# Audio tower on one core: the matrix work of a group laid out over its half units, the router in single steps

## The reference, cut to what matters

```python
h = tok(x, ...)                       # conv 2 -> 32 channels, width 7; 16 samples folded; 64 x 128 x 256
h = h + mamba(layernorm(h), ...)      # x_inner, z = x @ W_in; conv over 4 steps; silu
                                      # delta = softplus(...); h_t = exp(delta*A) * h_t-1 + delta*B*x
                                      # y = sum_n h*C + D*x; y * silu(z); @ W_out
h = h + moe(layernorm(h), ...)        # 8 experts, the two with the largest softmax gates
                                      # out = sum over the two: gate * (silu(x @ wg) * (x @ wi)) @ wo
```

## Time and profile before

| | us |
|---|---|
| median of 3 runs | 3025.95 (3023.35 to 3029.46) |
| the profiled execution | 3023.12 |
| its span in the profile | 3021.4 |
| busy: TensorE, VectorE, GpSimd, ScalarE | 2618.3, 2159.1, 1727.5, 1470.0 |
| matmuls of the state sums (L1215) | 1053.1 |
| scans (L899), idle just before them | 1172.5, 114.3 |
| products with C (L907) | 625.9 |
| delta*x*B on GpSimd (L514) | 1157.4 |

### The profile page before, as it was taken

One profiled execution on the slowest core, in us unless ns is written; L12 is line 12 of the kernel. 1 busy time (PEld: TensorE's weight loads), 2 busy tenths in 40 slices (PEclk: granted clock), 3 DMA queues, 4 the chain that ended last, 5 costly groups with the idle time before them and its releaser, 6 DMA issues. The chain is left out here.

```text
span 3021.4 us, 29407 instructions
## 1 busy us (share of the span) xinstructions
PE 2618.3 (87%) x7774; PEld 1298.5 (43%) x7775; DVE 2159.1 (71%) x2367; ACT 1470.0 (49%) x2717; POOL 1727.5 (57%) x864
## 2 busy tenths in 40 slices
PE   4689798887979889898888989877569999999999
PEld 2234343343434334343343434333246666666665
DVE  0599998999999999999999999999632222222222
ACT  1665656656566665656666566665212222222222
POOL 1567768677786867768677776877322222222222
PEclk9899998999999999899999989999889999999999
DMA  1321403223040321404123040321522222222222
GB/s 38 127 97 42 145 26 129 75 86 131 23 146 29 132 99 55 143 15 142 60 100 130 24 146 29 129 109 42 188 61 44 44 45 44 44 45 43 44 44 31
DMA packets 125603, 236.12 MB, mean 78 GB/s; under 512 B 46450, under 2 KB 93715, under 8 KB 109123
## 3 DMA queue, kind: packets, MB, share of 16 engines
q1 hardware_dynamic: 98342, 200.56, 19.5%
q0 software_dynamic: 26128, 34.36, 6.6%
q10 hardware_dynamic: 1036, 0.09, 0.0%
HBM read 182.22 MB, written 53.78 MB: 78 GB/s over the span
## 5 line engine op out<-in xcount | busy, mean ns | idle before, releaser
L514 POOL TENSOR_TENSOR arena<-u,arena 128x2048 f32<-128x2048 f32 x256 | 1157.4, 4527 | 368.4 <-DVE psum L899 366.9
L1215 PE MATMUL psum<-hc,ident 128*128 128x512 f32 x2048 | 1053.1, 641 | 263.2 <-DVE hc L907 262.5
L899 DVE TENSOR_TENSOR_SCAN psum<-psum,arena 128x1024 f32<-128x1024 f32 x512 | 1172.5, 2290 | 114.3 <-ACT psum L705 79.4
L1215 PEld LDWEIGHTS psum<-hc,ident 128*128 128x128 f32 x2048 | 382.3, 200 | 817.3 <-DVE hc L907 450.2
L705 ACT ACTIVATE psum<-delta,a_neg 128x508 f32<-128x508 f32 x1024 | 656.5, 674 | 0.6
L907 DVE TENSOR_TENSOR hc<-psum,arena 128x1024 f32<-128x1024 f32 x512 | 625.9, 1222 | 15.4
L588 POOL DMA_INDIRECT out_dram<-hres,tok_id x136 | 211.1, 1552 | 599.2 <-ACT hres L837 549.3
L1346 PE MATMUL psum<-arena,xnt 128*128 x1088 | 514.2, 595 | 0.0
L1101 DVE COPY z<-psum 128x512 f32<-128x512 f32 x136 | 94.0, 691 | 457.5 <-PE psum L1355 457.5
L837 ACT ACTIVATE hres<-psum,tok_w 128x256 f32<-128x256 f32 x136 | 64.4, 473 | 454.4 <-PE psum L1365 447.7
L1365 PE MATMUL psum<-arena,z 128*128 x1088 | 257.1, 379 | 0.9 <-DVE z L1101 0.9
(11 more groups left out here) (145 smaller groups left out, 1923.4 us busy)
## 6 DMA issues: line engine op xcount, KB each, us to landing
arena<-ssm_rows SPq DMA_DIRECT2D x128, 1024.0 KB, 5.8
delta<-expert_rows SPq DMA_DIRECT2D x136, 129.0 KB, 2.1
h_saved_rows<-hnew SPq DMA_DIRECT2D x16, 512.0 KB, 6.7
hres<-h_saved_rows SPq DMA_DIRECT2D x16, 512.0 KB
out_dram<-h SPq DMA_DIRECT2D x16, 512.0 KB, 2.9
draw<-ssm_rows SPq DMA_DIRECT2D x16, 256.0 KB, 3.1
arena<-in_L_ffn_wg_dram SPq DMA_DIRECT2D x8, 512.0 KB
arena<-in_L_ffn_wi_dram SPq DMA_DIRECT2D x8, 512.0 KB
```

Of the source, the lines that this page charges most:

```text
L514: pool.tensor_tensor(dBx[k % 2], rep, b_rep[:, q * QN:(q + 1) * QN, :], ALU.mult).then_inc(dbx_ready, 1)
L899: nc.vector.tensor_tensor_scan(h, h, src, 0.0, ALU.mult, ALU.add).then_inc(scan_done, 1)
L1215: last = nc.tensor.matmul(yacc[(k // HC) % 2], ident[:, :], hc[k % 2][:, i, :], start=False, stop=(k % HC == HC - 1 and i == 1))
```

## The change

TensorE: the first three projections of z of a group move from `k` = 0 to 2 of its own step to `k` = 29 to 31 of the step before (group 0: into the front, ahead of softplus on ScalarE), the fourth from 3 to 1; the output projection moves from 4, 5, 6, 7 to 2, 3, 6, 9; turning of the normed rows from 5, 6 to 3, 4; the first projection of x from 7 to 5 with its convolution at 7 and 8; the turned rows of the second norm from 14, 15 to 17, 18, the logits from 16 to 19, the counts from 21 to 27. ScalarE's evacuations follow; its first norm is cut in two (k = 1 and 2), Silu of z goes from 8 to 9, the four Abs are one per half unit (23 to 26), Exp and Ln go from 26 and 27 to 27 and 28, Relu to 26, 29, 30, 31.

VectorE: the router becomes 19 operations, one or two per half unit from 20 to 29, on both sides of `times_c`; it works on logits less their maximum, the first gate is the reciprocal of the sum of exponentials, the second that times `esecond`, an exponential of the second largest that ScalarE makes (`second_gate`). Its scratch is all in PSUM, over ten slices of `bank_b`. The mask is gone: `count` adds both one-hots (28 matmuls of 8 columns rather than 14). The residual additions stand at 4 and 10 ahead of `times_c`, statistics and their aggregation in different half units.

GpSimd: additions, products and `rsqrt` one per unit, and both scatters of a group are two groups behind (units 2, 3 and 5, 6), so that all scatters of the last group but one move to the tail.

The core of the diff:

```diff
+                pool.wait_ge(second_exp, g + 1)
+                pool.tensor_tensor(row[:, :, C + 1:C + 2], einv[:, :].rearrange("p (b a) -> p b a", a=1),
+                                   esecond[:, :].rearrange("p (b a) -> p b a", a=1), ALU.mult).then_inc(second_set, 1)
...
-                    if k in (0, 1, 4):
-                        c = {0: 1, 1: 2, 4: 3}[k]
+                    if k == 0 and not last:
+                        rsqrt(g + 1, 0, stat1, pow1)
+                    if k in (1, 4, 8):
+                        c = {1: 1, 4: 2, 8: 3}[k]
                         add_delta(g, c)
                         make_u(g, par, c)
                     if not second:
-                        if k == 0:
+                        if k == 2:
+                            first_row(g - 2)
+                        if k in (2, 3):
+                            scatter(g - 2, 0, 2 * (k - 2))
+                        if k == 5:
                             second_row(g - 2)
-                        if k in (1, 2):
-                            scatter(g - 2, 1, 2 * (k - 1))
-                    if k == 0 and not last:
-                        rsqrt(g + 1, 0, stat1, pow1)
-                    if not first:
-                        if k == 5:
-                            rsqrt(g - 1, 1, stat2, pow2)
-                        if k == 12:
-                            first_row(g - 1)
-                        if k in (13, 14):
-                            scatter(g - 1, 0, 2 * (k - 13))
-
-            def tail(g):
-                second_row(g - 1)
-                scatter(g - 1, 1, 0)
-                scatter(g - 1, 1, 2)
-                rsqrt(g, 1, stat2, pow2)
+                        if k in (5, 6):
+                            scatter(g - 2, 1, 2 * (k - 5))
+                    if k == 7 and not first:
+                        rsqrt(g - 1, 1, stat2, pow2)
...
+                nc.scalar.activation(r_ex, r_sub, ACT.Exp).then_inc(lexp_ready, 1)
+
+            def second_gate(g):
+                actq.wait_ge(dv, ROUTER * g + 7)
+                ahead(actq, second_set, g)
+                nc.scalar.activation(esecond[:, :], second[:, :], ACT.Exp).then_inc(second_exp, 1)
...
+                for c in range(NCH - 1):
+                    evac_z(0, c)
+                for c in range(NCH):
+                    softplus_abs(0, c)
...
-                    if k == 31 and not last:
-                        softplus_relu(g + 1, 3)
                     if k + 1 < HU:
                         exps(g, k + 1)
                     elif not last:
+                        softplus_relu(g + 1, 3)
                         exps(g + 1, 0)
-                    if k < NCH:
-                        evac_z(g, k)
+                    if not last and k in (1, 2):
+                        norm1(g + 1, k - 1)
+                    if k == 2:
+                        evac_z(g, 3)
+                    if k == 9:
+                        silu_z(g)
                     if not last:
-                        if k == 3:
-                            norm1(g + 1)
-                        if k in (5, 6):
-                            evac_xnt(g + 1, k - 5)
-                        if k in (7, 10, 13, 16):
-                            evac_xi(g + 1, (k - 7) // 3)
-                        if k in (9, 12, 15, 18):
...
-                    if k == 8:
-                        silu_z(g)
+                        if k in (3, 4):
+                            evac_xnt(g + 1, k - 3)
+                        if k in (5, 10, 13, 16):
+                            evac_xi(g + 1, (5, 10, 13, 16).index(k))
+                        if k in (8, 12, 15, 18):
+                            evac_conv(g + 1, 1 - par, (8, 12, 15, 18).index(k))
                     if not first:
-                        if k in (12, 13):
-                            norm2(g - 1, k - 12)
                         if k in (14, 15):
-                            evac_xn2t(g - 1, k - 14)
-                        if k == 17:
+                            norm2(g - 1, k - 14)
+                        if k in (17, 18):
+                            evac_xn2t(g - 1, k - 17)
+                        if k == 21:
                             router_exp(g - 1)
+                        if k == 26:
+                            second_gate(g - 1)
...
-                        if k in (24, 25):
-                            softplus_abs(g + 1, k - 24)
-                        if k == 26:
+                        if k in (23, 24, 25, 26):
+                            softplus_abs(g + 1, k - 23)
+                        if k == 27:
                             softplus_exp(g + 1)
-                        if k == 27:
+                        if k == 28:
                             softplus_ln(g + 1)
-                            softplus_relu(g + 1, 0)
-                        if k == 28:
-                            softplus_relu(g + 1, 1)
-                            softplus_relu(g + 1, 2)
+                        if k in (26, 29, 30):
+                            softplus_relu(g + 1, (26, 29, 30).index(k))
+                        if k in (29, 30, 31):
+                            evac_z(g + 1, k - 29)
...
+            def first_keys(g):
+                dve.wait_ge(lexp_ready, g + 1)
+                nc.vector.scalar_tensor_tensor(out=r_key, in0=r_sub, scalar=0.0, in1=key_w[:, :, :],
+                                               op0=ALU.is_ge, op1=ALU.mult).then_inc(dv, 1)
+
+            def largest_key(g, n):
+                after(g, n)
+                nc.vector.tensor_reduce(kmax[:, :], r_key, AX_X, ALU.max).then_inc(dv, 1)
+
+            def one_hot(g, n, k, done):
+                after(g, n)
+                nc.vector.tensor_tensor(oh[:, k, :, :], r_key, bc(kmax[:, :]), ALU.is_equal).then_inc(done, 1)
+
+            def without_first(g):
+                after(g, 4)
+                nc.vector.scalar_tensor_tensor(out=r_rest, in0=oh[:, 0, :, :], scalar=-1.0e30, in1=r_sub,
+                                               op0=ALU.mult, op1=ALU.add).then_inc(dv, 1)
+
+            def exp_sum(g):
+                nc.vector.tensor_reduce(esum[:, :], r_ex, AX_X, ALU.add).then_inc(dv, 1)
+
+            def second_max(g):
+                after(g, 5)
+                ahead(dve, second_exp, g)
+                nc.vector.tensor_reduce(second[:, :], r_rest, AX_X, ALU.max).then_inc(dv, 1)
...
+            def exp_inverse(g):
+                after(g, 6)
+                ahead(dve, second_set, g)
+                nc.vector.reciprocal(einv[:, :], esum[:, :]).then_inc(dv, 1)
...
+            def second_equal(g):
+                after(g, 7)
+                nc.vector.tensor_tensor(r_eq, r_rest, bc(second[:, :]), ALU.is_equal).then_inc(dv, 1)
+
+            def second_keys(g):
+                after(g, 9)
+                nc.vector.tensor_tensor(r_key, r_eq, key_w[:, :, :], ALU.mult).then_inc(dv, 1)
...
+                    if not first:
+                        if k == 4:
+                            residual(g - 1, 0)
+                        if k == 10:
+                            residual(g - 1, 1)
+                        if k == 20:
+                            router_max(g - 1)
+                        if k == 22:
+                            first_keys(g - 1)
+                        if k == 23:
+                            one_hot(g - 1, 3, 0, dv)
+                        if k == 24:
+                            second_max(g - 1)
+                            exp_inverse(g - 1)
+                        if k == 25:
+                            second_keys(g - 1)
+                        if k == 26:
+                            one_hot(g - 1, 11, 1, mask_ready)
+                        if k == 28:
+                            positions(g - 1)
+                        if k == 29:
+                            slots(g - 1)
+                    if k == 30 and more:
+                        aggregate(g + 2, 0, stat1)
                     times_c(g, k)
                     if not first:
-                        if k == 6:
-                            residual(g - 1, 0)
-                        if k == 9:
-                            residual(g - 1, 1)
+                        if k == 10:
                             stats2(g - 1)
-                        if k == 17:
-                            router_a(g - 1)
-                        if k in (19, 20):
-                            for part in ((0, 1), (2,))[k - 19]:
-                                router_b(g - 1, part)
+                        if k == 11:
+                            aggregate(g - 1, 1, stat2)
+                        if k == 20:
+                            router_sub(g - 1)
                         if k == 22:
-                            router_c(g - 1)
-                    if k == 28 and more:
+                            largest_key(g - 1, 2)
+                        if k == 23:
+                            without_first(g - 1)
+                            exp_sum(g - 1)
```

(50 more changed lines are left out.)

152 lines of the change are left out of this document (71 added, 81 removed).

## The result

The changed kernel takes **2897.26 us** (median of 4, 2895.21 to 2898.09), the kernel before beside it 3024.65: ratio 0.9578, 95% interval 0.9565 to 0.9591. That is 127 us less; 104 were forecast. 2897 lies in the stated range (2892 to 2974), near its lower end, but outside the 2900 to 2950 that the forecast gave its own sum, and nearer to rival 2 (2894) than to the forecast (2922). The profiled execution took 2897.52 us, its span is 2895.8 (before 3021.4).

A forecast was written before the change was run, and what follows sets the result against it. VectorE was taken to set the scan phase's pace. Front +11, group 0 -3, fourteen middle groups -105 (-7.5 each), last group -7, tail -1.4 and +1.5: -104 from 3025.95, 2922 us; own range 2900 to 2950, with rivals 2892 to 2974.

The forecast's parts named there:

- rival 2: Middle groups: nearly all stalls go, -9.5 us a group, 2894 us in all; chance 0.09.
- the slots' prices: VectorE small operations: 0.23 us when chained, 0.10 apart behind times_c, free between scan and times_c; -4.4 us a group together.
- The stalls at k=4, 8 and 9: Middle groups: k=4 (GpSimd) goes, -1.1 us; k=8 and 9 (TensorE's lag) go, -2.8 us.
- The stall at k=21: Middle groups: the chain around Silu of x stays, uncovered by router work; stall 2.3 us instead of 0.6.
- The front: Before the first scan: three z evacuations ahead of ScalarE's Abs, each behind its matmuls, +11 us.
- Rival 1: Stalls come to as much as before at other places; only VectorE's 4.4 us a group count, 2971 us; chance 0.20.
- rival 3: A small VectorE operation costs 0.23 us wherever it stands; only the six removed count, 2960 us; chance 0.04.
- rival 4: Half clock under z's matmuls from k=29: no change (3025) or slower (+51 us); chance 0.03 same, 0.05 slower.
- The 0.45 at k=26: Middle groups: one Abs instead of two ahead of the exponentials cuts the stall from 1.17 to about 0.45 us.
- The 0.5 for half clock under z: z's matmuls at k=29 to 31 meet half clock at times: 0.5 us a group, bounds 0 and 7.
- the 0.4 of small gaps: Middle groups: small stalls on VectorE left as before, 0.4 us a group.
- the bound of +12: Tail: GpSimd must send eight scatters before rsqrt while weights load; taken as +1.5 us, bounds 0 and +12.

The follow-up runs named there:

- experiment 2: Kernel before with the new router in single steps, nearly all other work in the old order: 2987.93 us, ratio 0.9883.
- experiment 3: Changed kernel with GpSimd's additions and products back at units 0, 1, 4 and first scatters at k=1, 2: 2923.54 us, ratio 0.9670.
- experiment 1: Changed kernel with the same 19 router operations gathered in four blocks behind times_c: 2933.79 us, ratio 0.9703.
- experiment 5: Kernel before with one filler matmul behind the turning of x at k=22 and 23: 3015.81 us, ratio 0.9959, executions in two clusters.
- experiment 8: Changed kernel with SyncE waiting for the earlier groups' scatters before asking for the weights of experts 2 to 8: 2897.8 us, ratio 0.9587.

## Why the prediction came out as it did

**Right.** VectorE sets the pace, and its work went by the slots' prices: the router's share fell from 5.1 to 1.07 us (forecast 1.1). The stalls at k=4, 8 and 9 went with the order that made them (experiment 2; the one at k=4 with GpSimd's part of it, experiment 3). The stall at k=21 came, and with its size: 2.22 for 2.3. The front gave +11.9 for +11, in the way described: two projections of 3.75 and 3.78 us, one of 1.99. Group 0, the last group, the router's chain in the tail (15.70 to 14.32) and the experts came out within half a microsecond each. Rival 1 fails on the stalls (2.45 left of 6.7), rival 3 on experiment 1, rival 4 on the clock, 1.00 from 229 to 1935 us. Rival 2, that nearly all stalls go, has the nearest number (2894, -9.5 us a group for the -9.36 measured) but not the mechanism: the stall at k=21 stayed with 2.2 us, and VectorE's work, which rival 2 takes as forecast, fell by another 0.5.

**The term that was mis-sized: what is left of the stalls in a middle group.** The sum put 3.65 us there, measured are 2.45: the 2.22 of k=21 and 0.23 in two small gaps. The 0.45 at k=26 rested on the step "one `Abs` instead of two ahead of the exponentials". That step had half of the mechanism: with both `Abs` the stall is there when the adding up of k=23 runs at half clock, and gone when it doesn't (two groups of the kernel before, experiments 2 and 5). The prediction counted the router's block at k=22 on VectorE alone; it also kept TensorE waiting, and the dip went with it. With the dip and the new order no stall is left at k=26 either (experiment 1), so either part of the change was enough there; whether that is the one `Abs` or the rest of the order is not shown. The 0.5 for half clock under z didn't come, and of the 0.4 of small gaps, carried over from before, 0.23 are there. That is 1.2 us. VectorE's work gave another 0.5 (11.7 to 6.8, 4.9 less, which was the bound): the router gave its 4.0, so the surplus is in the residual additions and the parted statistics, 0.9 us for 0.4. Together 1.7 us in the group shown, and 1.86 in the mean of the 14, some of which were slower before than the one shown: 26 us.

**The term that was missed: a wait in the tail.** Scatters were costed at +1.5 by what they do to GpSimd's `rsqrt`. That was nearly so: it starts 2.3 us behind its statistics (2047.77, VectorE), where before it started at once. But the norm behind it also waits for the scatters to land, since it writes the buffer that they read, 2.6 us more: from statistics to norm it takes 6.8 us where before took 2.0. The prediction asked who stands behind the scatters in GpSimd's queue, and not who waits for their landing. Less the 1.4 that the router's chain gives, and with 0.5 in pieces, that is +3.9 where +0.1 was put; the bound of +12 covered it. Experiment 8 shows that it is no gain to be fetched by waiting: there the weights come in the way of the last scatters instead.

The misses have opposite signs, -26 and +4, and add up to the 22 us by which the span differs from the forecast. The mechanism of the forecast holds in its main parts; that 2897 still lies in the range is owed to a range wide enough for half of rival 2. One piece of the gain has more behind it than the reason given, the stalls at k=26 and 27, 22.3 us in the kernel before.

## What to carry to other kernels

On an engine that sets the pace, ask of each small operation not only what it lasts but what is in flight when it is issued: between a long operation and the one that needs it, it is free; behind one that it doesn't need, a tenth; in a chain, more than twice that. A chain that makes a stall may need no shortening, only one more step of distance from the burst ahead of it (24.5 us here for three numbers). And look for half clock where the engine that sets the pace will wait for the slow matmuls, not where the clock is low for longest: at a group's end 0.50 cost nothing here, one adding up at half clock cost 1.4 to 3.1 us a group. A block of small operations on one engine can be what makes another wait long enough for that. Last, two experiments that each leave out one part of a change don't add up to it unless one of them has what the other lacks; here both kept the shorter router.

## What the runs showed of the hardware

- The granted clock fell to its lower level (1.2 of 2.4 GHz) behind an idle stretch of TensorE of 2.40 us (before, at 973.96) and behind one of 2.01 us (before with the filler, at 1027.91). It stayed at 2.4 GHz behind one of 2.40 us (before, at 585.97) and one of 2.08 us (before, at 1293.49). So in these traces the length of the one gap doesn't say whether the clock falls. With the first gap filled the clock fell in the next one, in ten of the 14 middle groups of the profiled execution; the executions of that kernel lie in two clusters, 12 us and more apart.
- A scatter issued from GpSimd while the weights load (382 GB/s, after) was held 7.30 us ahead of its issue, and GpSimd then waited 5.48 us for the four to land. With no weights in flight (experiment 8) the same scatter was still held 3.44 us, and the wait for the landing was 1.57.
- ScalarE's switch of tables costs the load alone, 1.28 us, with the activation starting 1.30 us after the load's start (910.62 to 911.92, 913.90 to 915.20).
- On VectorE an operation behind a scan of 2.29 us that doesn't need its result starts 2.20 us after the scan's start (920.00 to 922.20); one that needs the scan's result starts after 2.33 (916.53 to 918.86).
